# Merged state-space scans: the input projection for the unit three ahead moved from the end of a unit's first slot to its front

## The reference

```python
xz = jnp.einsum('bhwc,ec->bhwe', x, in_w)
xa, z = jnp.split(xz, 2, axis=-1)
xc = silu(dwconv3x3(jnp.transpose(xa, (0, 3, 1, 2)), conv_w, conv_b))
...
x_dbl = jnp.einsum('bkdl,kcd->bkcl', xs, xproj_w)      # xs: xc in four directions k
dts = jnp.einsum('bkrl,kdr->bkdl', x_dbl[:, :, :R], dt_w)
delta = jax.nn.softplus(dts + dt_b[None, :, :, None])
...
h = a * h + bu                                          # a = exp(delta*A), bu = delta*B*x
return (h, jnp.einsum('bkdn,bkn->bkd', h, c))
...
yo = layernorm(yo, ln_g, ln_b) * silu(z)
return jnp.einsum('bhwd,cd->bhwc', yo, out_w)
```

## Time and profile before

| | us |
|---|---|
| median of 3 runs | 7986.28 |
| lowest and highest run | 7963.08, 7991.41 |
| the profiled execution: its time | 7985.33 |
| the profiled execution: its span | 7983.4 |
| busy TensorE, VectorE, ScalarE, GpSimd over the span | 6266.9, 6478.1, 5242.1, 5481.8 |

### The profile page before, as it was taken

One profiled execution on the slowest core, in us unless ns is written; L12 is line 12 of the kernel. 1 busy time (PEld: TensorE's weight loads), 2 busy tenths in 40 slices (PEclk: granted clock), 3 DMA queues, 4 the chain that ended last, 5 costly groups with the idle time before them and its releaser, 6 DMA issues. The chain is left out here.

```text
span 7983.4 us, 105067 instructions
## 1 busy us (share of the span) xinstructions
PE 6266.9 (78%) x18336; PEld 2181.2 (27%) x18336; DVE 6478.1 (81%) x7496; ACT 5242.1 (66%) x10803; POOL 5481.8 (69%) x4416
## 2 busy tenths in 40 slices
PE   6878887677887785478888888888888777888686
PEld 2222222122222221122222222222222113488242
DVE  6998999779999997289999999999999994533636
ACT  6777777567777774366777777777777763222646
POOL 5888888668888885078888888888888981000606
PEclk8888888788888887688999999888888888997888
DMA  3444444344444444277777777777777772246312
GB/s 90 105 95 96 102 107 98 77 93 106 106 98 96 105 107 112 88 185 175 178 180 180 181 180 183 178 180 177 178 178 178 183 169 83 83 157 191 87 48 73
DMA packets 580429, 1050.78 MB, mean 132 GB/s; under 512 B 101719, under 2 KB 136812, under 8 KB 575180
## 3 DMA queue, kind: packets, MB, share of 16 engines
q1 hardware_dynamic: 580140, 1047.89, 54.6%
HBM read 858.09 MB, written 189.54 MB: 131 GB/s over the span
## 5 line engine op out<-in xcount | busy, mean ns | idle before, releaser
L1579 POOL TENSOR_TENSOR scan_prod<-scan_hs,scan_BC_rep 128x512 f32<-128x512 f32 x1536 | 1939.9, 1271 | 442.7 <-DVE scan_hs L1503 437.3
L600 POOL TENSOR_TENSOR mamba_prod<-mamba_hs,mamba_BC_rep 128x512 f32<-128x512 f32 x1536 | 1930.0, 1268 | 387.4 <-DVE mamba_hs L552 359.1
L552 DVE TENSOR_TENSOR_SCAN mamba_hs<-mamba_dA,mamba_carry,mamba_dbx 128x512 f32<-128x512 f32 x1152 | 1463.8, 1271 | 0.0
L1128 PE MATMUL scan_u_rep<-scan_du,scan_sel 96*128 96x512 f32 x1536 | 969.7, 717 | 472.9 <-DVE scan_hs L1503 472.1
L491 ACT ACTIVATE mamba_dA<-mamba_delta_rep,mamba_a_neg 128x512 f32<-128x512 f32 x1536 | 1090.2, 711 | 133.5 <-DVE mamba_hs L552 132.1
L1353 ACT ACTIVATE scan_dA<-scan_delta_rep,scan_a_neg 128x512 f32<-128x512 f32 x1536 | 1092.1, 712 | 90.4 <-DVE scan_hs L1503 77.7
L1503 DVE TENSOR_TENSOR_SCAN scan_hs<-scan_dA,scan_carry,scan_u_rep 128x512 f32<-128x512 f32 x768 | 976.6, 1272 | 161.0 <-ACT scan_carry L1333 157.6
L539 DVE TENSOR_TENSOR mamba_dbx<-mamba_u_rep,mamba_BC_rep 128x512 f32<-128x512 f32 x1152 | 788.8, 685 | 317.8 <-PE mamba_u_rep L314 132.1
L1503 DVE TENSOR_TENSOR_SCAN scan_hs<-scan_dA,scan_carry,scan_dbx_even 128x512 f32<-128x512 f32 x768 | 976.2, 1271 | 34.2 <-ACT scan_carry L1333 31.5
L282 PE MATMUL mamba_pre<-mamba_h,mamba_w_conv 96*96 96x512 f32 x1024 | 588.6, 715 | 324.2 <-POOL mamba_tails L568 272.5
L1890 POOL TENSOR_TENSOR ffn_sq<-ffn_xm 96x512 f32<-96x512 f32 x64 | 66.2, 1035 | 1030.5 <-DVE ffn_xm L1858 1019.7
(11 more groups left out here) (283 smaller groups left out, 10783.0 us busy)
## 6 DMA issues: line engine op xcount, KB each, us to landing
scan_BC_rep<-proj_rows SPq DMA_DIRECT2D x1024, 256.0 KB, 6.4
scan_delta_rep<-proj_rows SPq DMA_DIRECT2D x1024, 192.0 KB, 3.5
mamba_BC_rep<-bc_units SPq DMA_DIRECT2D x256, 512.0 KB, 10.3
mamba_delta_rep<-delta_units SPq DMA_DIRECT2D x512, 192.0 KB, 3.6
proj_rows<-scan_dbc SPq DMA_DIRECT2D x256, 224.0 KB, 2.6
delta_units<-mamba_delta SPq DMA_DIRECT2D x128, 192.0 KB, 6.3
by_n<-fin_res SPq DMA_DIRECT2D x32, 768.0 KB, 3.2
fmid_src<-by_n SPq DMA_DIRECT2D x32, 768.0 KB, 5.1
```

Of the source, the lines that this page charges most:

```text
L552: nc.vector.tensor_tensor_scan(hs[:, s % RING_H], dA[:, s % RING_A], dbx_bank(s)[:], carry[:, bass.ds(at, 1)], op0=ALU.mult, op1=ALU.add). ...
L600: pool.tensor_tensor(prod[:, (G * u + s) % RING_P], hs[:, s % RING_H], BC_rep[:, u, QUADS + s % QUADS], ALU.mult).then_inc(s_prod, 1)
L1128: nc.tensor.matmul(u_rep[c][:], sel[:, c], du[:, k], start=True, stop=True).then_inc(s_rep_u, 1)
L1579: pool.tensor_tensor(prod[:, (G * k + s) % RING_P], hs[:, (G * k + s) % RING_H], BC_rep[:, k, 2 + s % 2], ALU.mult).then_inc(s_prod, 1)
```

## The change

`project` and its waits are called ahead of the other work of slot 0, no longer behind it. Nothing is added or taken away.

```diff
                     for s in range(G):
                         q = G * j + s
                         at = G * k + s
+                        if ahead and s == 0:
+                            pe.wait_ge(s_bc, j + PRE)
+                            pe.wait_ge(s_relu, j + PRE)
+                            project(lay if k + PRE < D else nxt_lay, kp, image, r, rows)
                         if s % 2 == 1 and (has_next or k + 1 < D):
...
                         if has_out and at == 21:
                             project_out(f, out)
 
-                        if ahead and s == 0:
-                            pe.wait_ge(s_bc, j + PRE)
-                            pe.wait_ge(s_relu, j + PRE)
-                            project(lay if k + PRE < D else nxt_lay, kp, image, r, rows)
                         if s in (1, 2) and not (isinstance(n, int) and n == 0 and k == 0):
```

## The result

The changed kernel takes 8019.49 us (median of 7 runs, 8003.72 to 8035.06), the kernel before 7982.86 us (median of 7, 7963.08 to 7991.41). The ratio of the runs is 1.005, with a 95% interval of 1.0037 to 1.0063: 0.5% slower; the medians lie 37 us apart. The forecast was 8010 against 7986, so 23.5 us more. The sign and the place were right, and the size fell short by a third.

The account below looks back on a forecast made before the run. VectorE was taken to bound the SS2D phase, pausing for ScalarE at slot 13. Slots 6, 12 and the clock counted 0, slot 0 cost 23.5 us: 7985.33 + 23.5 = 8008.8, median 8010 us; range 7965 to 8045.

Parts of the forecast that it names:

- What bounds the kernel: SS2D phase: VectorE, 93% busy, sets the pace; it waits 189.1 us for ScalarE, at slot 13, after the ninth tap.
- Slot 6: Projection ahead of the fifth tap: arrives about 0.9 us sooner, ScalarE then waits longer for the ninth tap; gain 0.
- Slot 12: Projection ahead of `mean`: TensorE free about 1.8 us sooner, `mean` moves by 0 to 0.1 us; cost and gain nothing.
- Slot 0: Projection ahead of `project_z`: ScalarE's copy of z and slot 2's `dA` come late, the scan 0.73 us late.
- 1.71 us later: Slot 0: `project_z`, now last, ends at 4440.07 in place of 4438.36; ScalarE's copy and next `dA` move as much.
- The term of 23.5 us: Loss at slot 2's scan: 29 iterations at 0.73 us plus 5 at 0.47 us; bounds 15 and 35 us.
- The clock as a second term: TensorE's clock in SS2D: longer idle ahead of slot 13, about 2.8 us in one piece, might lower it; no cost forecast.
- The rival as written: Slots 21 to 0: second stretch's clock pattern spreads to the first, costing 38 us; median 8032 us, chance 0.18.
- the third: Sign that the prediction is wrong: iterations in the first stretch become irregular; no size given.
- The faster one: Slot 6: earlier projection is felt, some 60 iterations win 0.9 us each; median 7956 us, chance 0.08.
- given back: No change: slot 13's pause shrinks by slot 2's loss, or second stretch leaves its slow pattern; about 7986, chance 0.16.

Follow-up runs that it names:

- f2: Kernel before, with the nine convolution taps in slots 1 to 8, two of them in slot 6: 7901.91 us, ratio 0.9903.
- e2: Kernel before, with the projection first in slots 6 and 12 only, old order in slot 0: 7994.57 us, ratio 1.0007.
- f6: f2 with the projection first in slot 6 alone: 7896.77 us, ratio 0.9901 to the kernel before.
- e3: Changed kernel, with ScalarE copying z in its slot 2 behind that slot's decay factor, not in slot 1: 7996.71 us, ratio 1.0012 to the kernel before.
- e5: Kernel before, TensorE's order kept, with ScalarE's copy of z made to wait for the projection that follows `project_z`: 8011.27 us, ratio 1.0044.
- e4: Kernel before, with ScalarE's copy of z moved to its slot 2 behind that slot's decay factor: 7987.37 us, ratio 0.9998.
- e1: Kernel before, with the projection ahead of `project_z` in slot 0 only, old order in slots 6 and 12: 8014.8 us, ratio 1.0038.
- f7: f2 with the projection first in slot 12 alone: 7880.15 us, ratio 0.9879 to the kernel before.
- f8: f2 with ScalarE's silu of the convolution behind the decay factor of slot 13 instead of ahead: 7964.18 us, ratio 0.9984 to the kernel before.

## Why the prediction was right, and where it fell short

**What bounds the kernel.** Right. VectorE's pause at slot 13 hangs on the ninth tap (f2 takes it from 159 to 39 us), and on the kernel before no order of the projections moves it: 160 us of it stand in the changed kernel. One reading was too broad: that the scans follow each other without a pause everywhere else held for the iteration followed, while over the phase VectorE also pauses ahead of slot 0, 32 us in 26 iterations (34 us in 33 with the change).

**Slot 6.** Right. ScalarE's wait moved from L1287 to L1266 by 38 to 67 us and nothing came of it (e2: 1.0007). With the later wait gone it is not nothing: f6 against f2 has pauses at slot 13 of 13 us in place of 39 us and a first stretch some 36 us shorter, and loses as much in the second stretch, so that the two medians agree by luck.

**Slot 12.** Right in the ordinary iterations, wrong on one sentence: in the last chunk of an image not "only the order changes". `mean` now ends behind the projection, ScalarE waits 16.9 us for it at L1307 in 8 iterations (3.5 us in 4 before), and VectorE pays about 4 us of it at slot 16. That is a term of the sum that I had put at 0.

**Slot 0.** The mechanism, the place and the pure price were right: e3 takes three quarters of the loss away by moving ScalarE's copy, and e5 gets 0.7 us in 21 iterations and 0.44 to 0.49 us in 7 from the delay alone. The step that failed is the size of the delay: "1.71 us later" took `project_z` at its duration in the earlier trace rows, 1.02 us, as if its place did not matter. At the end of the slot it took 1.89 us in 10 iterations, so that ScalarE was 2.6 us late and VectorE 1.6 us. The pair of matmuls then took 3.66 us (4114.09 to 4117.75) where at full clock it took 2.80 us (4522.09 to 4524.89): "TensorE's last instruction of a slot 0 ends where it ended" held at full clock alone. The term of 23.5 us measured 27 to 30 us between slots 0 and 2. The rest of the 38 us is the late `mean`, 4 us, and small differences at slots 0 and 13 and in the steps after slots 15 and 16. An edit that does nothing moves the phase by as much (e4's, 3176.4 us, is 5 us longer), so I do not divide it further. The number of iterations came near by other places than foretold: 27 pauses for 34, with 16 in the first stretch for 22.

**The clock as a second term.** I had named it, and put 0 in the forecast and 0.18 on a rival. The rival as written (the pattern of the second stretch spreads to the first, with low clock on the output projection) did not come about as such: the first stretch has 50.8 us and not 51.2 us. What came is low clock at another place, slot 0. The Trainium skill's rule (TensorE: Matmul & The Clock Gate, section HAM oscillation — how this bites in real kernels) is that idle time between bursts of matmuls brings the clock down again and again. The trace agrees only in so far as the clock is down at slot 0 in ten iterations of the changed kernel (0.72 over the 8 us from 4111); that idle time brings it down there is not shown. The idle piece ahead of slot 13, to which I had applied the rule, is not the cause: e1, where it is short, has the loss and 7 slow `project_z`. Of the three signs of being wrong that the prediction named, the third came: the iterations of the first stretch, 49.2 to 50.0 us before, now vary from 50.0 to 52.0 us from one start of L1277 to the next. But e4, whose edit does nothing, has single iterations of 51.1 us there as well, so this sign says little about the change.

**The rivals.** The faster one was refuted by e2, and "given back" by the unchanged pause at slot 13 and the unchanged second stretch. Of the sizes foretold for the profile, 27 new waits of VectorE (foretold some 30), 126.7 us for z (near 100), -66.6 us at L1287 (-55), +47.5 us at L1266 (as much), and the gone wait ahead of `mean` came as written or near it; the length of VectorE's pauses, 0.3 to 0.84 us in 17 and 1.5 to 1.7 us in ten, did not (0.5 to 0.7).

## What to carry to other kernels

Before two pieces of work trade places in one engine's queue, look at who takes each result first, and at what stands behind the taker in its own queue: here a piece needed three slots later was put ahead of one for which ScalarE stood waiting, with the next scan's factor behind it. A wait that gets shorter brings nothing as long as a later wait of the same engine ends at the same event; find the event (the ninth tap) and move that, which brought 1% to 1.2%. And a matmul's duration belongs to its place: when it is moved to another point of a loop it may meet TensorE's other clock, so take its price at both. And equal medians do not show that an edit did nothing: f6's agreed with f2's by a gain and a loss of some 36 us each, in different stretches.

## What the runs showed of the hardware

- **The handover from ScalarE to a VectorE that stands idle took 0.30 us** from the end of the decay factor to the start of the scan, in 54 of the 55 pauses of slot 13 in the kernel before and in 26 of the 27 pauses of slot 2 with the change (4526.21 to 4526.51 us; 4413.17 to 4413.46 us in e5). It is not one number for the pair of engines: in f7's 28 pauses at slot 16, after 0.90 to 1.16 us of idle time, it took 0.14 us. What makes the difference is not shown.
- **A projection that reads columns took 1.8 times as long as one that reads rows, and only at full clock**: two fp32 matmuls took 1.87 us where direction 3 reads the image by columns, 1.02 us where direction 0 reads it by rows, at the same full clock. At 1.2 GHz both took 1.91 us. In the kernel before, a projection by columns in slot 12, then one by rows in slot 6 of iteration 58, and the windows around both, with the clock (0.50) behind the busy times:

```profile
4018.62 1.91 PE L1102 MATMUL scan_pre<-scan_xc,scan_w_proj 96*112 x2
6305.40 1.91 PE L1102 MATMUL scan_pre<-scan_xc,scan_w_proj 96*112 x2
4018.60:4020.60 2.00, 1.93 (x3) 0.31 (x1) 0.70 (x1) 1.99 (x6) 0.00 (x0) 0.50 1.00 223
6305.40:6307.40 2.00, 1.92 (x3) 0.31 (x1) 2.00 (x3) 0.04 (x1) 1.76 (x2) 0.50 0.31 101
```

  So a low clock costs almost nothing where the projection by columns stands, and 0.87 us where `project_z` stands.
- **Whole stretches of a loop settle into one of two paces**, in f2 to f8 with a granted clock of 0.89 to 0.93 or of 0.83, and with up to 4 us difference in an iteration of 47 to 51 us. One edit of TensorE's order, slot 6 alone (f6), moves the second stretch from one to the other, from 48.7 to 51.1 us, while its median says that nothing happened. I had not expected that a loop keeps such a state over 16 iterations, nor that it would outweigh the edit itself.
